# A mixture of experts in three-part fp32: the first matmul by one level of Strassen

## The reference

```
xn = xf / rms * norm_weight                                  # 8192 x 512
logits = xn @ router_weight.T + router_bias
_, idx = top_k(logits.T, 512)                                # 16 x 512
xe = xn[idx]                                                 # 16 x 512 x 512
h = einsum('ecd,efd->ecf', xe, fc1_weight) + fc1_bias        # F = 2048
h = gelu(h, approximate=False)
y = einsum('ecf,edf->ecd', h, fc2_weight) + fc2_bias
contrib = y * gates
output = zeros.at[flat_idx].add(contrib)                     # then divided by the gate sums; x is added
```

## Time and profile before

| | |
|---|---|
| median of 3 runs | 2315.03 us (2313.16 to 2316.53) |
| profiled execution: span | 2316.8 us (no time of its own stands beside it) |
| busy: TensorE, weight loads | 2080.0 us (90%), 1744.4 us (75%) |
| busy: VectorE, ScalarE, GpSimd | 1314.2 us (57%), 885.5 us (38%), 682.0 us (29%) |
| experts' stage, first matmul of an expert to the end | 816.5 to 2316.8 us |

### The profile page before, as it was taken

The page is one execution under the profiler, slowest core; times in us unless marked ns, Lnnn a source line. Parts: engine busy times, 40 slices in busy tenths (PEclk is TensorE's granted clock), DMA queues, the critical chain, the costliest instruction groups (busy, mean ns, idle before and its releaser), DMA issues.

```text
span 2316.8 us, 33321 instructions
## 1 busy us (share of the span) xinstructions
PE 2080.0 (90%) x11030; PEld 1744.4 (75%) x11030; DVE 1314.2 (57%) x2139; ACT 885.5 (38%) x1508; POOL 682.0 (29%) x648
## 2 busy tenths in 40 slices
PE   0889999999932199999999999999999999999997
PEld 0778888888821178888888888888888888888885
DVE  5678888878757544454453544545535445445353
ACT  2334444444400044443444444444444444444433
POOL 1434443444400122322421323223213232242131
PEclk9888998988855589999999999999999999999998
DMA  3741111111162244343443443434434434343343
GB/s 141 253 155 56 57 57 52 63 59 54 58 205 91 76 165 127 110 109 112 126 109 110 110 127 110 109 113 125 109 110 110 127 110 109 114 124 109 110 109 73
DMA packets 92819, 251.87 MB, mean 109 GB/s; under 512 B 19393, under 2 KB 20609, under 8 KB 92033
## 3 DMA queue, kind: packets, MB, share of 16 engines
q1 hardware_dynamic: 75426, 215.90, 28.1%
q0 software_dynamic: 17376, 35.77, 8.3%
HBM read 212.26 MB, written 56.11 MB: 116 GB/s over the span
## 4 chain that ended last, share of the span: by engine, by line
PE 64%; POOL 0%; issue 0%; DVE 0%; DMA 0%; ACTq 0%; ACT 0%; POOLq 0%; DVEq 0%
PE experts_b_h L249 10%; PE experts_b_h L251 10%; PE experts_b_h L250 10%; PE experts_b_y L250 10%; PE experts_b_y L249 10%; PE experts_b_y L251 10%; PE experts_b_list L1466 2%; PE experts_b_x L1475 1%; POOL out L1335 0%; PE experts_b_y L1475 0%; DMA experts_rows<-xn_dram,experts_rows_id 0%; POOL experts_rows_meta L1307 0%; POOL experts_rows L1316 0%; DMA experts_rows_meta<-meta_dram,experts_next_ids 0%; DVE experts_named L1407 0%
## 5 line engine op out<-in xcount | busy, mean ns | idle before, releaser
L1449 DVE TENSOR_TENSOR experts_h_lo<-experts_h,experts_h_hi 128x512 fp32r<-128x512 f32 x256 | 182.1, 711 | 691.2 <-ACT experts_h_hi L1380 691.2
L1377 ACT ACTIVATE experts_h<-experts_b_h,experts_b_sb 128x512 f32<-128x512 f32 x256 | 176.4, 689 | 796.4 <-PE experts_b_h L251 796.4
L249 PE MATMUL experts_b_h<-experts_xT_hi,experts_w_hi 128*128 x1024 | 413.5, 404 | 1.7 <-DVE experts_xT_lo L1425 1.7
L251 PE MATMUL experts_b_h<-experts_xT_hi,experts_w_lo 128*128 x1024 | 408.0, 398 | 0.0
L250 PE MATMUL experts_b_h<-experts_xT_lo,experts_w_hi 128*128 x1024 | 406.6, 397 | 0.0
L250 PE MATMUL experts_b_y<-experts_w_lo,experts_h_hi 128*128 128x512 f32 x1024 | 400.6, 391 | 0.0
L249 PE MATMUL experts_b_y<-experts_w_hi,experts_h_hi 128*128 128x512 f32 x1024 | 400.0, 391 | 0.0
L251 PE MATMUL experts_b_y<-experts_w_hi,experts_h_lo 128*128 128x512 f32 x1024 | 399.5, 390 | 0.0
L1389 DVE TENSOR_TENSOR experts_w_lo<-experts_w_raw,experts_w_hi 128x1024 fp32r<-128x1024 f32 x258 | 327.0, 1268 | 59.5 <-ACT experts_w_hi L1357 59.4
L1357 ACT ACTIVATE experts_w_hi<-experts_w_raw 128x1024 fp32r<-128x1024 f32 x258 | 269.9, 1046 | 120.5 <-DMA experts_w_raw<-in_w 120.5
L1335 POOL DMA_INDIRECT out<-experts_y_out,experts_ids x64 | 115.1, 1798 | 568.6 <-DVE experts_y_out L1433 554.0
(11 more groups left out here) (282 smaller groups left out, 3315.7 us busy)
## 6 DMA issues: line engine op xcount, KB each, us to landing
experts_w_raw<-in_w SPq DMA_DIRECT2D x258, 512.0 KB, 3.3
attend_bias_raw<-in_bias SPq DMA_DIRECT2D x76, 256.0 KB, 3.1
xn_dram<-g_in_row SPq DMA_DIRECT2D x1, 16384.0 KB, 47.3
attend_q_x<-in_x SPq DMA_DIRECT2D x20, 256.0 KB, 2.7
attend_k_x<-in_x SPq DMA_DIRECT2D x20, 256.0 KB, 2.7
xn_dram<-attend_xn SPq DMA_DIRECT2D x18, 256.0 KB, 2.0
experts_b_sb<-in_b SPq DMA_DIRECT2D x1, 4096.0 KB, 12.5
lists_wq_raw<-in_wq SPq DMA_DIRECT2D x1, 2048.0 KB, 12.2
```

The lines of the kernel that those rows point to most:

```text
L249: nc.tensor.matmul(out, lh, rh, start=first, stop=False)
L251: return nc.tensor.matmul(out, ll, rh, start=False, stop=last)
L1377: nc.scalar.activation(h[:, f % HB, :], b_h[f % 2][:, :], ACT.Gelu, bias=b1[:, bass.ds(e, 1), f].rearrange("p o -> p o")).then_inc(h_done, 1)
L1449: nc.vector.tensor_tensor(h_lo[:, f % HB, :], h[:, f % HB, :], f32(h_hi[:, f % HB, :]), ALU.subtract).then_inc(h_lo_ready, 1)
```

## The change

Pairs of chunks are computed together, in 8 periods q per expert. Of a pair's 256 hidden features, 512 inputs and 512 tokens each is cut into halves, so fc1 of a pair is a product of 2x2 blocks A (weights) and B (tokens): A is 256 features x 512 inputs, B is 512 inputs x 512 tokens. By Strassen's rule in Winograd's form it is formed from seven products of half-size blocks instead of eight. A half-size product (`product`) is 2 input blocks x 3 matmuls of 256 columns.

- The sums of weight blocks S1 to S4 are made by GpSimd (`weight_sums`, four operations of 128x256) into one buffer `s_raw`, for each pair, from `w1_raw` (fc1's weights now have a DMA of their own, 512 KB per pair and 2 slots; fc2's are another). ScalarE and VectorE split three raw blocks (768 elements) and four sums (1024).
- The sums of token blocks T1 to T4 are made by GpSimd once per expert (`x_first`, `x_others`, four operations of 512) in the tensor `y` that is free then, from a copy `x_raw` of the transposed tokens; the splits are one operation of 1536 and one of 2048 elements on each of ScalarE and VectorE.
- The products gather in three banks `b_a`, `b_b`, `b_c`. ScalarE copies three intermediate states of 256 columns to SBUF (`p1_copy`, `p5_copy`, `u2_copy`); VectorE adds three blocks of h from a copy and a bank; the fourth is read from PSUM by gelu.
- TensorE's order in a period: three products, fc2 of the pair before for token block 0, and then products and fc2 groups in turn.
- GpSimd's queue gets a `weight_sums` ahead of each step; the list for expert e+2 is made in the period after expert e, and fetches use lists made an expert earlier.
- `bias_w` is gone: VectorE adds the bias b2 to y (`base_row`) and ScalarE multiplies by the weight (`scale_row`), in the first period of the next expert; b2 is loaded for one expert at a time.

```
+    A11, A12, A22, S1, S2, S3, S4 = range(7)
+    B11, B22, B21, T1, T3, T2, T4 = range(7)
+    RAW_B12, RAW_B11, RAW_B22, RAW_B21 = range(4)
...
+        s_raw = sb("s_raw", [P, 4, 2 * P])
+        w1_hi = sb("w1_hi", [P, 2, 7, 2 * P], F32R)
+        w1_lo = sb("w1_lo", [P, 2, 7, 2 * P], F32R)
...
+        h = sb("h", [P, 2, CAP])
+        h_hi = sb("h_hi", [P, 2, 2, CAP], F32R)
+        h_lo = sb("h_lo", [P, 2, 2, CAP], F32R)
+        p1_copy = sb("p1_copy", [P, HALF])
+        p5_copy = sb("p5_copy", [P, HALF])
+        u2_copy = sb("u2_copy", [P, HALF])
...
+                def weight_sums(turn, g, slot):
+                    pool.wait_ge(w1_in[slot], (turn + 1) * 16)
+                    if not (isinstance(g, int) and g == 0):
+                        pool.wait_ge(w1_lo_done, g * 2)
+                    alone(pool, passed)
+                    a21, a11, a12, a22 = [w1_raw[:, slot, n, :] for n in range(4)]
+                    s1, s2, s3, s4 = [s_raw[:, n, :] for n in range(4)]
+                    nc.gpsimd.tensor_tensor(s1, a21, a22, ALU.add).then_inc(s_done, 1)
+                    nc.gpsimd.tensor_tensor(s3, a11, a21, ALU.subtract).then_inc(s_done, 1)
+                    pool.wait_ge(s_done, g * 4 + 1)
+                    nc.gpsimd.tensor_tensor(s2, s1, a11, ALU.subtract).then_inc(s_done, 1)
+                    pool.wait_ge(s_done, g * 4 + 3)
+                    nc.gpsimd.tensor_tensor(s4, a12, s2, ALU.subtract).then_inc(s_done, 1)
...
+                weight_sums(1, 2, 0)
+                with pool.Fori(0, E - 1) as e:
+                    for q in range(2, Q + 2):
+                        weight_sums(e * (Q // 2) + (q + 1) // 2, e * Q + (q + 1), (q + 1) % 2)
+                        if q == 2:
+                            adopt(e)
+                            fetch_meta(e + 1)
+                        elif q == 3:
+                            fetch_rows(e + 1)
+                        elif q == 5:
+                            x_first(e + 1)
+                        elif q == 6:
+                            x_others(e + 1)
                     add_rows(e)
-
                     pool.wait_ge(y_added, (e + 1) * CT * 16)
                     alone(pool, passed)
...
+                def split_w1_sums(g, slot):
+                    act.wait_ge(s_done, (g + 1) * 4)
+                    nc.scalar.activation(w1_hi[:, slot, 3:7, :], s_raw[:, :, :], ACT.Copy)\
+                        .then_inc(w1_hi_done, 1)
...
+                def period(e, q, g, turn, ahead=True, middle=(), end=()):
+                    slot = q % 2
+                    act.wait_ge(product_done, g * 7 + 1)
+                    nc.scalar.activation(p1_copy[:, :], b_a[:, 0:HALF], ACT.Copy).then_inc(copy_done, 1)
+                    act.wait_ge(product_done, g * 7 + 2)
+                    nc.scalar.activation(p5_copy[:, :], b_b[:, 0:HALF], ACT.Copy).then_inc(copy_done, 1)
+                    if ahead:
+                        split_w1_raw(turn + (1 if q % 2 else 0), 1 - slot)
+                        split_w1_sums(g + 1, 1 - slot)
+                    act.wait_ge(product_done, g * 7 + 4)
+                    nc.scalar.activation(u2_copy[:, :], b_a[:, 0:HALF], ACT.Copy).then_inc(copy_done, 1)
+                    for extra in middle:
+                        extra()
+                    act.wait_ge(w2_in[slot], (turn + 1) * 16)
+                    if not (isinstance(g, int) and g == 0):
+                        act.wait_ge(fc2_done, g)
+                    nc.scalar.activation(w2_hi[:, slot, :], w2_raw[:, slot, :], ACT.Copy).then_inc(w2_hi_done, 1)
+                    if q == 0:
+                        act.wait_ge(b1_ready, e + 1)
+                    act.wait_ge(sum_done, g * 3 + 2)
+                    nc.scalar.activation(h[:, 0, :], h[:, 0, :], ACT.Gelu,
+                                         bias=b1_now[:, 2 * q:2 * q + 1]).then_inc(gelu_done, 1)
+                    act.wait_ge(gelu_done, g * 3 + 1)
+                    nc.scalar.activation(h_hi[:, slot, 0, :], h[:, 0, :], ACT.Copy).then_inc(h_hi_done, 1)
...
+                    period(e + 1, 0, e * Q + Q, e * (Q // 2) + Q // 2,
+                           end=tuple(lambda c=c: scale_row(e, c) for c in range(CT)))
...
+                    nc.vector.tensor_tensor(y[:, c, :], b_y[c][:, :], b2[:, :], ALU.add).then_inc(y_based, 1)
...
+                    nc.vector.tensor_tensor(h[:, 0, 0:HALF], p1_copy[:, :], b_c[:, 0:HALF], ALU.add)\
+                        .then_inc(sum_done, 1)
+                    if ahead:
+                        split_w1(g + 1, 1 - slot)
+                    dve.wait_ge(product_done, g * 7 + 5)
+                    dve.wait_ge(copy_done, g * 3 + 3)
+                    nc.vector.tensor_tensor(h[:, 0, HALF:CAP], u2_copy[:, :], b_b[:, 0:HALF], ALU.add)\
+                        .then_inc(sum_done, 1)
+                    dve.wait_ge(product_done, g * 7 + 6)
+                    nc.vector.tensor_tensor(h[:, 1, HALF:CAP], p5_copy[:, :], b_a[:, 0:HALF], ALU.add)\
+                        .then_inc(sum_done, 1)
+                    dve.wait_ge(w2_hi_done, g + 1)
+                    nc.vector.tensor_tensor(w2_lo[:, slot, :], w2_raw[:, slot, :], f32(w2_hi[:, slot, :]), ALU.subtract)\
...
+                    period(0, e * Q + Q, middle=(lambda: name(e + 2), lambda: base_row(e, 0)),
+                           end=tuple(lambda c=c: base_row(e, c) for c in range(1, CT)))
...
+                def product(target, slot, w, side, x, first, last_in):
+                    for k in range(2):
                         cols = slice(k * P, (k + 1) * P)
+                        left_hi, left_lo = w1_hi[:, slot, w, cols], w1_lo[:, slot, w, cols]
+                        right_hi = x_hi[:, bass.ds(side, 1), x, k, :].rearrange("p o t -> p (o t)")
+                        right_lo = x_lo[:, bass.ds(side, 1), x, k, :].rearrange("p o t -> p (o t)")
+                        for i, (left, right) in enumerate(((left_hi, right_hi), (left_hi, right_lo), (left_lo, right_hi))):
+                            last = nc.tensor.matmul(target[:, 0:HALF], left, right, start=first and k == 0 and i == 0,
+                                                    stop=last_in and k == 1 and i == 2, skip_group_check=True)
+                    last.then_inc(product_done, 1)
+
...
+                def fc2_first(e, q, g):
+                    pe.wait_ge(w2_lo_done, g + 1)
+                    pe.wait_ge(h_lo_done, g * 2 + 1)
+                    fc2(e, q, 0, 0)
+                    pe.wait_ge(h_lo_done, g * 2 + 2)
+                    fc2(e, q, 1, 0)
+
+                def period(e, q, g, side, rows=None, after_c0=None, after_p4=None):
+                    slot = q % 2
+                    if rows is not None:
+                        pe.wait_ge(gelu_done, g * 3)
+                    if q == 0:
+                        pe.wait_ge(x_lo_ready, e * 2 + 1)
+                    pe.wait_ge(w1_lo_done, g * 2 + 1)
+                    product(b_a, slot, A11, side, B11, True, False)
+                    if q == 0:
+                        pe.wait_ge(x_lo_ready, e * 2 + 2)
+                    pe.wait_ge(w1_lo_done, g * 2 + 2)
+                    product(b_b, slot, S1, side, T1, True, False)
+                    product(b_c, slot, A12, side, B21, True, True)
+                    if rows is not None:
+                        fc2_first(rows[0], rows[1], g - 1)
+                    if after_c0 is not None:
+                        after_c0()
+                    pe.wait_ge(copy_done, g * 3 + 1)
+                    product(b_a, slot, S2, side, T2, False, False)
+                    if rows is not None:
+                        fc2(*rows, 0, 1)
+                    pe.wait_ge(copy_done, g * 3 + 2)
+                    product(b_b, slot, S4, side, B22, False, True)
+                    pe.wait_ge(copy_done, g * 3 + 3)
+                    product(b_a, slot, S3, side, T3, False, False)
+                    if rows is not None:
+                        fc2(*rows, 1, 1)
+                        fc2(*rows, 0, 2)
+                    pe.wait_ge(sum_done, g * 3 + 3)
+                    product(b_a, slot, A22, side, T4, False, True)
+                    if after_p4 is not None:
+                        after_p4()
+                    if rows is not None:
+                        fc2(*rows, 1, 2)
+                        fc2(*rows, 0, 3)
+                        fc2(*rows, 1, 3)
...
+                    for q in range(1, Q):
+                        after_c0, after_p4 = None, None
+                        if q in (4, 5):
+                            after_c0 = lambda: turn_next(e + 1, (q - 4) * 2)
+                            after_p4 = lambda: turn_next(e + 1, (q - 4) * 2 + 1)
+                        period(e, q, e * Q + q, side, (e, q - 1), after_c0, after_p4)
+                    side = pe.snap((e + 1) % 2)
+                    period(e + 1, 0, e * Q + Q, side, (e, Q - 1), lambda: list_after(e + 2))
```

(5 more changed lines are left out.)

466 lines of the change are left out of this document (296 added, 170 removed).

## The result

The changed kernel takes 2412.45 us (median of four runs, 2410.35 to 2414.51), the kernel before 2315.78 us (2313.16 to 2323.55): ratio 1.041, with a 95% interval of 1.038 to 1.044. Forecast were 2370 us and slower: the sign and the first of the two places came true, the size was +96 us instead of +55. The time lies in the stated range of 2280 to 2420 us, near its upper end, and just above the range that the forecast gave itself (2330 to 2410).

What follows compares the result with a forecast made beforehand. TensorE was taken to bound the experts' stage. TensorE's gain -92, 14 boundaries +141, the last +5, start +6 and end -5 gave +55 us: 2370 us, stated range 2280 to 2420, the forecast's own 2330 to 2410.

Steps and rivals of the forecast that it cites:

- What bounds it, and what TensorE gains: Experts' stage: TensorE sets the time; 42 matmuls at 0.117 us save 0.72 us per pair, 92 us in all (76 to 102).
- Other engines within a period: Ordinary period of 10.4 us: ScalarE about 7 us, VectorE 6.1 us, so it stays TensorE's and these edits cost nothing.
- The scatter, the set and the first stop: Period 2 of an expert: weight sums behind the scatter's landing ready at T = 18.9, wanted at 14.7; TensorE waits 4.2 us.
- The second stop: Period 3: sums behind adopt and meta gathers ready at T = 32.9, wanted at 25.1; 7.8 us late in all.
- After it nothing long stands in the queue and GpSimd catches up: GpSimd's queue after the row fetch and the set for period 4, that set 8.0 us late: no further lateness.
- Period 0: Second product of an expert's first period: split token sums ready at about 11.5, wanted at 11.1; 0.8 us taken (0 to 2).
- A boundary's total: Turn from expert to expert: 8.0 lateness, 0.3 of period 9, 0.8 token sums and 1.0 clock, in us, at 14 boundaries.
- Start and end: Experts' stage: its start costs about +6 us (3 to 12), its end gives -5 us.
- the rival in which the clock stays low: After each boundary stop the clock falls and stays low: 3.4 us counts instead of 1, about 2405 us; chance 0.13.
- The one with a shorter queue: GpSimd's queue from first scatter to period 3's set is shorter: 3.4 us late, 2280 us, change faster; chance 0.25.
- late in every period: VectorE, sharing tensors with GpSimd, late by 0.3 us on 128 periods: 38 us, 2410 us; chance 0.07.
- the weight load is not hidden at all: 256-column fc1 matmuls at the 0.158 us load pace: fc1 +128 us, about 2540 us; chance 0.05.

Runs made afterwards that it cites:

- experiment 9: The changed kernel with every matmul of a product but the first narrowed from 256 to 128 token columns: 2408.49 us in one run.
- experiment 1: The changed kernel with GpSimd's first set of weight sums ahead of the wait for the scatter's landing: 2351.01 us, ratio 1.015.
- experiment 5: The changed kernel with GpSimd's order rewritten: ids and weights held in copies, both sets of sums and all fetches ahead of the landing wait: 2283.11 us, ratio 0.988.
- experiment 6: experiment 5 with VectorE reordered: token sums' low halves ahead of w2's, list parts at ends of periods 2 to 5: 2270.59 us, ratio 0.981.
- experiment 8: experiment 6 with the long list part at the end of period 1, the first at 3, the others at 4 and 5: 2261.82 us, ratio 0.977.
- experiment 2: The changed kernel with the four weight sums of each pair on VectorE, none on GpSimd: 2353.25 us, ratio 1.015.

## Why the prediction was right, and where its size was off

- *What bounds it, and what TensorE gains.* Right in kind. The pace was 0.120, not 0.117, and fc2 0.231 in the mean where 0.229 was taken: a period is 10.55 us instead of 10.4. The gain is 4.5 us per expert instead of 5.8: over 16 experts about 20 of the 41 us that are missing. The bound (76 us) was right, the choice inside it was not; half of the 512-column pace would have been 0.1175, and experiment 9 shows that the pace does not halve with the columns.
- *Other engines within a period.* Right: periods 1, 5 and 7 have no gap. The copies of 256 took 0.38 us (0.4 estimated).
- *The scatter, the set and the first stop.* The scatter started at T = 1.0 as forecast; its stretch took 15.7 us, not 14.1, and the set 2.9, not 3.8 with its issue; ready at T = 19.6 against 18.9, a stop of 4.6 us (4.3 in the mean) against 4.2. Experiment 1 takes it away alone, so the cause is shown.
- *The second stop.* Forecast at T = 32.9, the sums end at 32.6; but TensorE lost only 0.8 us there in the mean instead of 3.8, and stood there under 0.3 us in ten of the 14 experts. The prediction itself names this as a sign that it is wrong ("if the second one is absorbed"), and in this step it was. The clock had been counted as 1 us, "behind the first stop the second absorbs it". It was the other way: the clock loss of 2.4 us came first and absorbed the second stop. That both together count once was right, and experiment 1 shows the second stop where the first is gone.
- *Not foreseen.* The token rows late for the turns of period 4 (1.4 us per expert), and the third sum late in period 6 behind two list parts in a row (0.7). I had said "After it nothing long stands in the queue and GpSimd catches up"; that step failed too. The row fetch was in the queue, but I compared it only with the set behind it and not with the turns, which want its landing. Experiment 5 shows it: with the rows fetched earlier period 4 takes 11.42 us instead of 12.85. For period 6, experiment 6: 10.55 instead of 11.26.
- *Period 0.* 0.8 us of gap for x_lo as forecast, 1.1 us longer by it; experiment 6 takes it away (13.75 to 12.69).
- *A boundary's total.* 10.7 us against 10.1 looks better than it is: the two stops with the clock took 7.4 us, where 9.0 were counted, the two stops not foreseen 2.1, where nothing was, period 0 took 0.4 more, and the 0.3 of period 9 was not lost. That these nearly cancel is luck.
- *Start and end.* The first product began 8.2 us later than the first matmul of fc1 before (824.68 against 816.51), with 3.0 us of gaps behind it; +6 was taken. Between kernels whose earlier stages are the same the first period begins anywhere from 818.6 to 831.8 us. What moves it stays open; it is the spread that limits all comparisons here.

Per expert this makes -4.5 + 10.7 = +6.2 us, where -5.8 + 10.1 = +4.3 was forecast: over the 14 inner experts +87 instead of +61. For the rest of the span +9 was measured, where the two outer experts' gain, the last boundary, start and end were to give -11.5 + 5 + 6 - 5 = -6. So of the 41 us some 20 are pace, 8 boundaries and 12 start and end. The total came near the price of the rival in which the clock stays low (2405), but not by its mechanism: the clock took 2.4 us per expert and 3.0 of the second stop's 3.8 were given back.

The other rivals. The one with a shorter queue was wrong for this kernel: a sum costs 0.72 us, not 0.5, and the stretch of the scatter was longer than taken. As a design it is right: with GpSimd's order rewritten the kernel takes 2283 us (experiment 5), with VectorE's too 2262 (experiment 8). VectorE is not late in every period: periods 1, 5 and 7 have no gap. That the weight load is not hidden at all is refuted at its price: the 0.158 us were busy time divided by loads, but the loads overlap each other; in the experts' stage a load's record is 0.19 us long, and the matmuls with their loads still start 0.120 us apart.

## What to carry to other kernels

When work is put into an engine's program that also waits for a DMA to land, its lateness is the whole of what stands ahead of it there, not its own 3 us. Before the arithmetic is changed, give the wait a place where nothing that the bounding engine wants is behind it (here a copy of ids and weights, and another order). And compare every instruction of the moved chain with each of its readers, not only with the next of its kind. A saving in columns is worth only what the pace of such matmuls shows: here 12.5% fewer columns gave 11% less fc1 time (42 x 0.120 against 24 x 0.235 us), and on the narrow side almost nothing.

## What the runs showed of the hardware

- With a new weight tile for each fp32r matmul, 512 columns took 0.227 to 0.236 us, 256 took 0.120 (0.115 in the attention) and 128 took 0.111.
- In the changed kernel a stop of 3.5 to 5.0 us went with a stretch at the granted clock 0.50, up to 6.8 us long, in all 14 inner experts. A stop of 2.3 us in experiment 1 did so in 8 of 13 experts (period 3 at 14.6 us or more) and not in the other five (13.1); the 14th had a stop of 5.7 and the fall. Stops of 1.6 to 2.4 us in experiment 2 did so in 4 of 11. The fall began during the stop or up to 1.5 us after it.
- A 0.72 us sum on GpSimd beside a 2.83 us VectorE operation ended only 0.6 us after it, in all 2.79 us (experiment 6); a low half of h of 0.69 took 2.91 beside four GpSimd sums (experiment 5):

```profile
1110.62 1.32 POOL L1354 TENSOR_TENSOR experts_s_raw<-experts_w_raw 128x256 f32<-128x256 f32 x1
...
1110.97 2.91 DVE L1652 TENSOR_TENSOR experts_h_lo<-experts_h,experts_h_hi 128x512 fp32r<-128x512 f32 x1
...
1112.31 1.02 POOL L1357 TENSOR_TENSOR experts_s_raw<-experts_s_raw,experts_w_raw 128x256 f32<-128x256 f32 x1
```

- The Trainium skill (SBUF — State Buffer, section "SBUF: two separate sides") has a GpSimd operation that reads SBUF and a VectorE operation with two SBUF inputs take one port pair for a whole instruction, whichever starts first, while the other stands; the 2.79 us agree. But the low half of h ended at 1113.88, 0.5 us after the third of the sums (1113.33): it was held by more than the one sum for which the prediction lets a low half wait at most. What decides which engine goes on after the first sum isn't shown.
- From the first of four scatters to the first instruction behind the wait for their landing the kernel needed 15.7 us in the expert shown and 15.4 in the mean, before 13.8 and 14.0; while GpSimd went on with sums and gathers (experiment 5) nothing waited for it any more.
